# Attention with each probability tile turned three slots behind its score in place of two

## The reference

```
q = query @ W_Query + B_Query
k = key @ W_Key + B_Key
v = value @ W_Value + B_Value
...
scores = jnp.einsum('bqhd,bkhd->bhqk', q, k) / D ** 0.5
probs = jax.nn.softmax(scores, axis=-1)
out = jnp.einsum('bhqk,bkhd->bqhd', probs, v)
out = out.reshape(B, Lq, H * D)
return out @ W_Output + B_Output
```

## Time and profile before

| | |
|---|---|
| median of 3 runs | 1860.14 us |
| profiled execution | 1861.19 us, its span 1859.5 us |
| mean granted TensorE clock | 0.943 |
| TensorE busy | 1683.3 us (91%) |
| VectorE busy | 1192.0 us (64%) |
| ScalarE busy | 842.8 us (45%) |
| GpSimd busy | 619.9 us (33%) |

### The profile page before, as it was taken

One profiled execution on the slowest core, in us unless ns is written; L12 is line 12 of the kernel. 1 busy time (PEld: TensorE's weight loads), 2 busy tenths in 40 slices (PEclk: granted clock), 3 DMA queues, 4 the chain that ended last, 5 costly groups with the idle time before them and its releaser, 6 DMA issues. The chain is left out here.

```text
span 1859.5 us, 26060 instructions
## 1 busy us (share of the span) xinstructions
PE 1683.3 (91%) x8890; PEld 1152.6 (62%) x8890; DVE 1192.0 (64%) x2642; ACT 842.8 (45%) x1870; POOL 619.9 (33%) x746
## 2 busy tenths in 40 slices
PE   6469999996999999999999999999999999873584
PEld 4357777764666666666666666666666666572352
DVE  6444454432777777777777777777777777667761
ACT  3324443431555555555555555555555555421110
POOL 2154444430333232333333233232323232210375
PEclk9669999997999999999999999999999999955797
DMA  7100000003323222232323223232322223144144
GB/s 258 21 22 13 12 12 1 1 0 105 69 46 69 53 61 64 51 69 46 69 48 67 56 58 68 46 69 46 68 51 64 58 57 69 23 146 132 44 85 57
DMA packets 66657, 109.46 MB, mean 59 GB/s; under 512 B 16088, under 2 KB 48096, under 8 KB 66528
## 3 DMA queue, kind: packets, MB, share of 16 engines
q1 hardware_dynamic: 60384, 99.29, 21.8%
q0 software_dynamic: 6144, 8.52, 2.8%
HBM read 27.84 MB, written 12.85 MB: 22 GB/s over the span
## 5 line engine op out<-in xcount | busy, mean ns | idle before, releaser
L1030 POOL TENSOR_SCALAR at_Pr<-at_Pr,at_rinv 128x512 f32<-128x512 f32 x512 | 354.1, 692 | 826.7 <-DVE at_rinv L1057 826.7
L1009 ACT ACTIVATE at_Pr<-at_ps,at_nmax 128x512 f32<-128x512 f32 x512 | 352.0, 687 | 522.7 <-DVE at_nmax L1052 521.1
L1052 DVE TENSOR_REDUCE at_nmax<-at_ps 128x1 f32<-128x512 f32 x512 | 350.9, 685 | 139.0 <-PE at_ps L917 128.0
L917 PE MATMUL at_ps<-at_k,at_q 128*128 128x512 f32 x1024 | 420.8, 492 | 9.7 <-DMA at_k<-at_k_own 8.0
L928 PE MATMUL at_ps<-k_ident,at_Pr 128*128 128x128 f32 x2048 | 310.5, 274 | 4.0 <-POOL at_Pr L1030 4.0
L928 PEld LDWEIGHTS at_ps<-k_ident,at_Pr 128*128 128x128 f32 x2048 | 249.5, 140 | 93.2 <-POOL at_Pr L1030 32.8
L1064 DVE COPY at_PT<-at_ps 128x512 f32<-128x512 f32 x384 | 261.3, 681 | 0.0
L917 PEld LDWEIGHTS at_ps<-at_k,at_q 128*128 128x128 f32 x1024 | 174.6, 191 | 129.6 <-issue 120.1
L938 PE MATMUL at_ps<-at_PT,at_V 128*64 128x512 f32 x1024 | 233.8, 598 | 0.9 <-DVE at_PT L1064 0.9
L1057 DVE RECIPROCAL at_rinv<-at_rsum 128x1 f32<-128x1 f32 x512 | 83.3, 163 | 174.5 <-ACT at_Pr L1009 172.5
L938 PEld LDWEIGHTS at_ps<-at_PT,at_V 128*64 128x64 f32 x1024 | 67.7, 136 | 121.5 <-issue 120.3
(11 more groups left out here) (237 smaller groups left out, 2030.5 us busy)
## 6 DMA issues: line engine op xcount, KB each, us to landing
at_k<-at_k_own SPq DMA_DIRECT2D x256, 256.0 KB, 4.1
k_x<-in_x SPq DMA_DIRECT2D x8, 512.0 KB, 7.8
mg_ctx<-in_ctx SPq DMA_DIRECT2D x8, 512.0 KB, 8.0
mx_ctxn<-in_ctx SPq DMA_DIRECT2D x8, 512.0 KB, 3.9
rows<-lo_xn SPq DMA_DIRECT2D x8, 512.0 KB, 3.0
out<-k_x SPq DMA_DIRECT2D x1, 4096.0 KB, 14.6
r_w<-in_L_ffn_w SPq DMA_DIRECT2D x16, 256.0 KB, 5.6
mx_w<-in_L_ffn_w SPq DMA_DIRECT2D x2, 1024.0 KB, 9.8
```

The source lines that it names most:

```text
L917: ins = pe.matmul(ps[:, S_BANK + j % 2, :], q2[:, u % 2, h, q:q + P], k2[:, u % 2, h, part, :], start=part == 0, stop=part == 1)
L1009: act.activation(Pr[:, j % 4, :], ps[:, S_BANK + j % 2, :], ACT.Exp, bias=nmax[:, j % 4:j % 4 + 1], accum_out=rsum[:, j % 4:j % 4 + 1]).th ...
L1030: pool.tensor_scalar(Pr[:, n % 4, :], Pr[:, n % 4, :], rinv[:, n % 4:n % 4 + 1], 1.0, ALU.mult, ALU.mult).then_inc(s["pn"], 1)
L1052: dve.tensor_reduce(nmax[:, j % 4:j % 4 + 1], ps[:, S_BANK + j % 2, :], AX.X, ALU.max, negate=True).then_inc(s["nmax"], 1)
```

## The change

`LAG = 3` takes the place of the number 2: the turn and the copy of tile j-3 stand in slot j. So the turns and the copies of tiles 5, 6 and 7 of unit u-1 lie in slots 0, 1 and 2 of unit u, and the value products of u-1 in slot 3, behind score 3 and turn 0. ScalarE copies tiles 2 and 4 in place of 4 and 5, in slots 5 and 7. `heads_out` in slot 4 moves behind the exponential. The number of instructions, their sizes, the buffers and the PSUM banks stay the same.

```diff
--- before.py
+++ after.py
@@ -849,7 +849,8 @@
                  "pt_v pt_a pv oT y_ps x")
         w_dram = [W.rearrange("(c p) n -> p c n", p=P) for W in (Wq, Wk, Wv)]
         wo_dram = Wo.rearrange("(a p) d -> p a d", p=P)
-        ON_ACT = (4, 5)
+        ON_ACT = (2, 4)
+        LAG = 3
         BY_ACT = [sum(j in ON_ACT for j in range(n)) for n in range(NBL + 1)]
         BY_DVE = [n - BY_ACT[n] for n in range(NBL + 1)]
 
@@ -956,13 +957,13 @@
                     for j in range(NBL):
                         if there(u):
                             score(u, j)
-                            if j >= 2:
-                                turn(u, j - 2)
-                        if j < 2 and there(u - 1):
-                            turn(u - 1, NBL - 2 + j)
+                            if j >= LAG:
+                                turn(u, j - LAG)
+                        if j < LAG and there(u - 1):
+                            turn(u - 1, NBL - LAG + j)
                         if j < 2 and there(u + 1):
                             project(u + 1, j)
-                        if j == 2 and there(u - 1):
+                        if j == LAG and there(u - 1):
                             weigh_values(u - 1)
                         if j == 4 and there(u + 1):
                             project_values(u + 1)
@@ -1001,14 +1002,14 @@
                 values(0)
                 for u in range(U + 1):
                     for j in range(NBL):
-                        if j == 4 and there(u - 1):
-                            heads_out(u - 1)
                         if there(u):
                             act.wait_ge(s["nmax"], NBL * u + j + 1)
                             wait_count(act, s["t_ps"], NBL * u + j - 3)
                             act.activation(Pr[:, j % 4, :], ps[:, S_BANK + j % 2, :], ACT.Exp,
                                            bias=nmax[:, j % 4:j % 4 + 1], accum_out=rsum[:, j % 4:j % 4 + 1]
                                            ).then_inc(s["exp"], 1)
+                        if j == 4 and there(u - 1):
+                            heads_out(u - 1)
                         if there(u + 1):
                             if j == 0:
                                 queries(u + 1)
@@ -1016,11 +1017,11 @@
                                 keys(u + 1)
                             if j == 5:
                                 values(u + 1)
-                        if there(u) and j - 2 in ON_ACT:
-                            act.wait_ge(s["t_ps"], NBL * u + j - 1)
-                            q = P * ((j - 2) % TPB)
-                            act.copy(PT[:, u % 2, (j - 2) // TPB, :, q:q + P],
-                                     ps[:, T_BANK + j % 2, :].rearrange("p (t q) -> p t q", t=TPB)
+                        if there(u) and j - LAG in ON_ACT:
+                            act.wait_ge(s["t_ps"], NBL * u + j - LAG + 1)
+                            q = P * ((j - LAG) % TPB)
+                            act.copy(PT[:, u % 2, (j - LAG) // TPB, :, q:q + P],
+                                     ps[:, T_BANK + (j - LAG) % 2, :].rearrange("p (t q) -> p t q", t=TPB)
                                      ).then_inc(s["pt_a"], 1)
 
             @block.gpsimd
@@ -1086,10 +1087,10 @@
                             if j >= 1:
                                 row_sum(u, j - 1)
                             row_max(u, j)
-                            if j >= 2:
-                                keep(u, j - 2)
-                        if j < 2 and there(u - 1):
-                            keep(u - 1, NBL - 2 + j)
+                            if j >= LAG:
+                                keep(u, j - LAG)
+                        if j < LAG and there(u - 1):
+                            keep(u - 1, NBL - LAG + j)
                         if there(u + 1):
                             if j == 1:
                                 queries(u + 1)
```

## The result

The changed kernel takes 1941.05 us, the median of 4 runs (1940.25 to 1944.11), against 1860.87 for the kernel before, measured beside it, also 4 runs: 1.0424 times as long, 95% interval 1.0401 to 1.0447. The profiled execution took 1944.11 us, with a span of 1942.4. It is slower by 80 us; the forecast was 77 (1937).

A forecast was written before the change was run, and what follows sets the result against it. TensorE, busy throughout, bounded the kernel at 18.16 us per unit; VectorE's late last copy would make it 19.39. 61 x 1.23 = 75 plus 1.3 for the ends, on 1861.19, gave 1937.5; predicted 1937, range 1910 to 1965.

The forecast's parts named there:

- TensorE's path: TensorE from one unit's value products to the next, summed from starts in the trace: ready again after 17.98 us.
- slot 2, now bare: 0.91: Slot 2 on TensorE, without value products: 0.91 us from turn 7 to turn 0, which starts at 17.45.
- the closest pair of score and exponential: Score j needs exponential j-2; closest named was score 0 at about 10.8 against the end of exponential 6 at 10.45.
- rival (a): Faster: last copy in time, only the turns' wait on GpSimd goes; 61 x 0.18 = 11 us, 1850; chance 0.05.
- a gain of 0.18 us per unit: TensorE's path alone, the wait on GpSimd gone: 18.16 - 17.98 = 0.18 us per unit.
- VectorE's stretch: VectorE, row maximum of slot 7 to last copy: stiff 8.75 us from 10.59; value products at 19.39, waiting 1.41.
- The cover of the last copy before: In the kernel before, VectorE's copy of tile 7 ended a full microsecond before the value products.
- The edits at no cost: ScalarE's copies, output eviction, probability buffers, score banks, key copies: no cost; the slot 5 copy has 0.1 us cover.
- The ends: Unit 0 about +1.4, unit without projections +0.4, last unit about -0.5: together +1.3 us, bounds -3 to +5.
- (b): VectorE's stretch starts earlier or has some give, say half the wait: 1890 to 1920 us; chance 0.08.
- (c): ScalarE's slot 5 queue delays exponential 6: up to 0.58 us per unit, at most 1973, likelier some 1960; chance 0.08.
- (d), the clock: TensorE's one wait per unit lowers its clock to a mean of 0.9: 70 us more, 2007; chance 0.04.

The follow-up runs named there:

- kernel 3: Changed kernel with the last copy (tile 7) first in VectorE's slot 2 and the query splits behind it in that slot: 1861.82 us over 12 runs.
- kernel 5: kernel 3 with ScalarE's query evictions also moved from slot 0 to slot 1, behind the exponential of tile 1: 1855.69 us over 8 runs.
- kernel 1: Changed kernel with VectorE's query splits moved from slot 1 to slot 2, behind the last copy: 1881.41 us.
- kernel 2: Changed kernel with the last copy first in VectorE's slot 2, query splits left in slot 1: 1890.25 us.
- kernel 4: Changed kernel with one unused 128x512 row maximum more on VectorE, directly in front of the copy of tile 7: 2005.94 us.
- kernel 9: Changed kernel with half a row maximum more (128x256) in front of the copy of tile 7: 1958.82 us over 2 runs.
- kernel 8: Kernel before with one additional row maximum in front of the copy of tile 7: 1861.01 us over 10 runs.
- kernel 7: Changed kernel with ScalarE copying tiles 3 and 4 in place of 2 and 4: 1940.5 us over 2 runs.
- kernel 11: Changed kernel with the output eviction back in front of exponential 4 on ScalarE: 1941.53 us over 2 runs.
- kernel 10: Changed kernel with two row maxima more in front of the copy of tile 7: 2086.55 us over 2 runs.

## Why the prediction was right

- **TensorE's path.** Seven of the eight turns lie within 0.02 us of where the prediction put them. Turn 0 is at 17.61, not 17.45: the prediction's "slot 2, now bare: 0.91" left out that score 3 needs exponential 1. I had compared the closest pair of score and exponential and named score 0; score 3 is closer (kernel 3). In the changed kernel the 0.16 us vanish in the wait that follows, which is so much shorter: 19.42 - 17.61 - 0.53 = 1.28 in place of 1.41. It had a price only in rival (a), and in the statement that the path alone is a gain of 0.18 us per unit: without the third edit of kernel 5 it is 0.04. The profile's idle record in front of the value products is 1.21 us, 73.2 in all; the 87.7 at the weight load come near the forecast 87 by chance.
- **VectorE's stretch.** Predicted 8.75 us, tied to TensorE at 10.59, with a release of 0.05: period 19.39. Measured 8.76, 10.60, 0.06: 19.40. Kernels 1, 2, 4 and 9 shortened and lengthened it by -1.00, -0.79, +0.60 and +0.33 us, and each time the period of the units at full clock followed to within 0.02 us. That its content is what matters, and not its distance to the value products, kernel 3 shows.
- **The cover of the last copy before.** A microsecond by the rows; 0.60 of it could be filled for nothing (kernel 8).
- **The edits at no cost.** ScalarE's copy in slot 5 rather than 6, and the order of its output eviction: none (kernels 7 and 11). The probability buffers, the score banks and the key copies weren't tried by themselves. No wait for the buffers or the key copies shows up in the full units; the score banks do hold score 3, as just said, and it costs nothing here because the later wait is longer.
- **The ends.** I put +1.3 us on them; they are 0.14 + 0.4. The +1.4 of unit 0 was too much: its value products waited 0.49 us by the record. Its stretch has no residual additions in it, as the prediction said; it still wrote down the whole wait. The first part of the stage (+1.55) and the part from the last value products on (+4.8) it left out.
- **Rivals.** (a), faster, needed the copy in time and would then have given 18.12, not 17.98, so no measurable gain: kernel 3. It takes a third edit, kernel 5 (1855.69 us). (b) and (c) are out, by the period and by kernel 7. (d), the clock, did not come in the full units at this wait, but its mechanism is real: it came at a wait 0.6 us longer. What held the clock in the changed kernel was a margin that I did not know, so that part of the forecast was luck. The Trainium skill (TensorE: Matmul & The Clock Gate, A second HAM failure mode) tells of such a going back and forth from short idles in every iteration; kernels 4 and 10 agree with it; kernel 9 and the changed kernel had idles of 1.54 and 1.21 us in every unit and kept the full clock.

The mechanism was right, and the period to 0.01 us. The total is less exact than that: the profiled execution took 1944.11 us for 1937.5, 6.6 more, which are 1.0 in the full units (76.0 for 75), -0.7 in the ends counted (0.56 for 1.3), 1.55 ahead of the first score and 4.8 behind the start of the last value products. The median of 1941, 4 us off, is nearer because this execution was the slowest of the four.

## What to carry to other kernels

A consumer's distance in slots is worth what the slowest queue in front of its input leaves of it: before an operation is moved later, find the last of its inputs in each engine's own order, and add up what stands in front of it there. A stretch that one engine runs without idling, tied at one point to the engine that sets the pace, can be carried over from the trace of before as one number; here it gave the new period to 0.01 us. And removing one wait from a chain shows the next one, 0.14 us behind it, only in the distance of starts, not in the waits view.

## What the runs showed of the hardware

The granted clock of TensorE can fall from a short idle that comes once in each period. With the same work on TensorE of some 18 us per unit, an idle record of 1.21 and 1.54 us in each unit left the clock at 1.00, 1.81 us brought it to the lower level at the value products in 16 of 61 units, and 2.40 us in 42 of 61, after 11 units at full clock. Each such unit cost 1.4 to 1.7 us more. So the price of a wait isn't linear: the 0.6 us of kernel 4 cost 1.05 us per unit, its share of the lower clock included. The length of one idle alone doesn't decide it either. In kernel 4 the units between the slow ones had the same 1.81 us. And in the last unit of the changed kernel TensorE stood idle for 1.29, 0.85 and 0.78 us with only a turn in between each, and the value products behind them took 5.35 us, while in the last unit of the kernel before 0.60, 0.95 and 0.89 us left them at 3.65.
